# FFN of a convolution-attention block: first layer as two fp16 products of split, DMA-turned rows, with the bias in ScalarE's copy

## The reference, cut to what matters

```
t = t + attn(ln(t))                      # gives x2
h = clip-scale(ln(t) @ sign(W1 - mean).T + b1)   # 96 -> 384, five groups of the batch
h = gelu(h)
t = t + clip-scale(h @ sign(W2 - mean).T + b2)   # 384 -> 96, five groups of the batch
```

## Time and profile before

| what | value |
|---|---|
| three runs | 2713.96, 2716.24, 2720.21 us, median 2716.24 |
| profiled execution | 2713.15 us, of which the trace spans 2711.4 us |
| mean granted TensorE clock | 0.977 |
| busy, share of the span | TensorE 93%, VectorE 78%, ScalarE 72%, GpSimd 56% |
| DMA bytes | 290.84 MB, mean 107 GB/s |

### The profile page before, as it was taken

The page is one execution under the profiler, slowest core; times in us unless marked ns, Lnnn a source line. Parts: engine busy times, 40 slices in busy tenths (PEclk is TensorE's granted clock), DMA queues, the critical chain, the costliest instruction groups (busy, mean ns, idle before and its releaser), DMA issues. The chain is left out here.

```text
span 2711.4 us, 83212 instructions
## 1 busy us (share of the span) xinstructions
PE 2534.1 (93%) x29309; PEld 1505.9 (56%) x29309; DVE 2103.7 (78%) x3025; ACT 1956.5 (72%) x3751; POOL 1509.3 (56%) x2545
## 2 busy tenths in 40 slices
PE   4899999999999959999999999999999997899996
PEld 2555555555555525666666666666666654455553
DVE  3577676666767448999999999999999975779997
ACT  2687777877777627777777777777777773677775
POOL 0133342333334247888888888888888871225445
PEclk9999999999999969999999999999999998999998
DMA  1122322323222246666666666666666634334546
GB/s 37 30 88 70 95 80 73 101 70 104 70 87 87 82 116 116 120 127 127 121 128 125 123 128 123 127 125 122 127 127 119 128 71 127 97 112 135 147 135 164
DMA packets 777485, 290.84 MB, mean 107 GB/s; under 512 B 702865, under 2 KB 760498, under 8 KB 777394
## 3 DMA queue, kind: packets, MB, share of 16 engines
q1 hardware_dynamic: 776050, 288.43, 46.6%
q10 hardware_dynamic: 1344, 1.18, 0.1%
HBM read 100.77 MB, written 87.29 MB: 69 GB/s over the span
## 5 line engine op out<-in xcount | busy, mean ns | idle before, releaser
L1034 DVE TENSOR_REDUCE at_row_max<-at_ps_queries 128x1 f32<-128x1024 f32 (+7 forms) x1536 | 1067.4, 745 | 103.9 <-PE at_ps_queries L917 103.9
L990 ACT ACTIVATE at_probs<-at_ps_keys 128x512 f32<-128x512 f32 x1344 | 720.8, 596 | 236.8 <-PE at_ps_keys L932 236.5
L907 PE MATMUL at_ps_queries<-at_turned 48*128 48x512 f16 (+3 forms) x2304 | 608.7, 332 | 58.5 <-DVE at_row_max L1034 36.4
L932 PE MATMUL at_ps_keys<-at_turned 50*128 50x128 f16 (+3 forms) x3456 | 574.8, 273 | 6.2 <-ACT at_diag_probs L990 0.5
L952 PE MATMUL at_ps_values<-at_probs,at_v 128*32 128x128 f32 x10752 | 413.8, 278 | 0.5 <-DVE at_out L1026 0.4
L932 PEld LDWEIGHTS at_ps_keys<-at_turned 50*128 50x128 f16 x3456 | 230.1, 94 | 195.0 <-ACT at_probs L990 74.4
L851 POOL TENSOR_TENSOR at_recip<-at_out,at_minus_one 128x8 f32<-128x8 f32 x192 | 313.7, 1634 | 2.8 <-DVE at_out L1026 2.8
L952 PEld LDWEIGHTS at_ps_values<-at_probs,at_v 128*32 128x32 f32 x10752 | 258.7, 109 | 89.9 <-issue 73.3
L513 POOL TENSOR_TENSOR cb_o_hat<-cb_o,cb_o_scale 128x768 f32<-128x768 f32 x32 | 48.0, 1501 | 461.5 <-DVE cb_o_scale L433 461.5
L990 ACT ACTIVATE at_diag_probs<-at_ps_keys 128x512 f32<-128x512 f32 x384 | 230.8, 601 | 35.9 <-PE at_ps_keys L932 27.7
L915 PE MATMUL at_ps_queries<-mask_queries,shifted 64*128 64x256 bf16 (+1 forms) x960 | 241.9, 252 | 0.0
(11 more groups left out here) (223 smaller groups left out, 5078.1 us busy)
## 6 DMA issues: line engine op xcount, KB each, us to landing
qkv_rows<-cb_packed SPq DMA_DIRECT2D x32, 1152.0 KB, 7.6
at_stacks<-qkv_rows SPq DMA_DIRECT2D x192, 192.0 KB, 2.9
cb_x<-in_x_dram SPq DMA_DIRECT2D x32, 384.0 KB, 3.7
cb_x_again<-in_x_dram SPq DMA_DIRECT2D x32, 384.0 KB, 4.5
x_after_conv<-cb_x SPq DMA_DIRECT2D x32, 384.0 KB, 5.0
ff_att_rows<-attention_rows SPq DMA_DIRECT2D x32, 384.0 KB, 4.3
ff_x<-x_after_conv SPq DMA_DIRECT2D x128, 96.0 KB, 2.3
x_after_attention<-ff_x SPq DMA_DIRECT2D x30, 384.0 KB, 2.9
```

The source lines that it names most:

```text
L907: mm = pe.matmul(scores[:, c0:c0 + width], QT[Q_ROWS, slot, qb * P:(qb + 1) * P], KT[Q_ROWS, slot, k0 * P:k1 * P], start=(c0 == 0), stop=True,
L932: mm = pe.matmul(pk[:, bank_k, c0:c0 + n * P], KT[K_ROWS, slot, kb * P:(kb + 1) * P], QT[K_ROWS, slot, q0 * P:(q0 + n) * P], start=(c0 == ...
L990: act.activation(probs, pk[:, ring(r, u + (u > MAX_TURN)), :], ACT.Exp, scale=scale).then_inc(S["probs"], 1)
L1034: ins = dve.tensor_reduce(MX[:, (r - 3) % 2, qb:qb + 1], pq[:, (NR * (r - 1) + g) % QBUFS, b0 * P:(b0 + n) * P], AX.X, ALU.max)
```

## The change

The float32 product becomes two fp16 ones. The sign weights are stored in fp16. GpSimd scales the normalised rows by 256 more than before (`XN_UNIT`, put in through the variance), copies them to fp16, subtracts that copy from the float32 rows and stores the remainder in fp16 too. A DMA transpose on SyncE's queue turns both parts; the eight TensorE transposes and ScalarE's copy of them go. The two parts are multiplied by the same weights into the same PSUM bank. b1 leaves the product and enters ScalarE's copy as a bias, with the scale 1/256. Everything ahead of the first layer runs one turn earlier (n = r + 3, m = r + 2).

```
-    w["w1"] = sb("w1", [C + 1, HIDDEN])
+    w["w1"] = sb("w1", [C, HIDDEN], FP16)
+    w["b1"] = sb("b1", [P, CHUNKS])
...
-        XNT = sb("xn_t", [C + 1, L])
+        XP = sb("xn_parts", [P, 2, TILES, P], FP16)
+        XNT = sb("xn_t", [P, 2, 2, TILES, P], FP16)
...
+                    if 0 <= x < FULL:            # SyncE, x = r + 1, behind the x2 store
+                        sp.wait_ge(S["xn_ready"], x + 1)
+                        _above(sp.wait_ge, S["y1_psum"], 6 * (x - 1))
+                        sp.dma_start_transpose(XNT[:, x % 2, :, :, :].rearrange("p m t n -> p (m t) n"),
+                                               XP[:, :, :, :].rearrange("p m t n -> p (m t n)")
+                                               ).then_inc(xn_turned[x % 2], 16)
...
-                        pe.matmul(pf[:, a * BANK:(a + 1) * BANK], w["w1"][:, k * P:(k + 1) * P],
-                                  XNT[:, a * BANK:(a + 1) * BANK], start=True, stop=True).then_inc(S["y1_psum"], 1)
+                        for part in range(2):
+                            tokens = XNT[0:C, n % 2, part, :, :].rearrange("p (e u) n -> p u e n", e=2)
+                            mm = pe.matmul(pf[:, a * BANK:(a + 1) * BANK], w["w1"][:, k * P:(k + 1) * P],
+                                           tokens[:, 2 * a:2 * a + 2, :, :], start=(part == 0), stop=(part == 1))
+                        mm.then_inc(S["y1_psum"], 1)
...
-                    if 0 <= r < FULL:
-                        pe.wait_ge(S["xn_ready"], r + 1)
-                        pe.wait_ge(S["att_copied"], min(r + 3, BATCH))
-                        for t in range(TILES):
-                            mm = pe.transpose(pt[0:C, t * P:(t + 1) * P], XN[:, t % 2 * 4 + t // 2, :], w["ident"][:, :])
-                        mm.then_inc(S["xn_turned"], 1)
...
-                                       ACT.Copy).then_inc(S["y1_copied"], 1)
+                                       ACT.Identity, bias=w["b1"][:, k:k + 1], scale=1.0 / XN_UNIT
+                                       ).then_inc(S["y1_copied"], 1)
...
-                        act.wait_ge(S["xn_turned"], r + 1)
-                        act.activation(XNT[0:C, :], pt[0:C, :], ACT.Copy).then_inc(S["xnt_ready"], 1)
...
                         pool.tensor_tensor(XN[:, :, :], XC[:, :, :], _bcast(SCALE[:, :], 2, C), ALU.mult
+                                           ).then_inc(S["xn_made"], 1)
+                        pool.wait_ge(S["xn_made"], m + 1)
+                        _above(pool.wait_ge, xn_turned[(m - 1) % 2], 16 * ((m + 1) // 2))
+                        pool.tensor_copy(XP[:, 0, :, 0:C], XN[:, :, :]).then_inc(S["xn_high"], 1)
+                        pool.wait_ge(S["xn_high"], m + 1)
+                        pool.tensor_tensor(XP[:, 1, :, 0:C], XN[:, :, :], XP[:, 0, :, 0:C], ALU.subtract
                                            ).then_inc(S["xn_ready"], 1)
```

More of the change, by code:

```diff
@@ L137, in prepare @@
             (w2_raw[:, :], A["L1_ffn_W2"]),
-            (w["w1"][C:C + 1, :], A["L1_ffn_b1"].rearrange("(a n) -> a n", a=1)),
+            (w["b1"][:, :], A["L1_ffn_b1"].rearrange("(k p) -> p k", p=P)),
             (lng[:, :], A["L0_conv_ln_g"].rearrange("(n a) -> n a", a=1)),
@@ L1048, in project_and_ffn @@
     LIMIT = QB - QEPS
+    XN_UNIT = 256.0
     FULL = GROUPS * GB
@@ L1077, in project_and_ffn @@
         G1, G2 = sb("max1", [P, 2, GB * CHUNKS]), sb("max2", [P, 2, GB])
-        ROW = sb("row_of_ones", [1, P])
+        ROW = w["fc1"][0:1, 0:P]
         M1, M2 = sb("group_max1", [P, GROUPS, 4]), sb("group_max2", [P, GROUPS, 4])
@@ L1101, in project_and_ffn @@
         stored = [sem(f"stored{i}") for i in range(4)]
-        names = ("ones_set half_set att_turned att_copied y_done x2_ready x2_turned x2_sums centred squares var_sums scale xn_ready "
-                 "xn_turned xnt_ready y1_psum y1_copied y1_max max1 all_max1 scale1 gelu h_ready y2_psum y2_ready "
+        xn_turned = [sem(f"xn_turned{i}") for i in range(2)]
+        names = ("ones_set half_set att_turned att_copied y_done x2_ready x2_turned x2_sums centred squares var_sums scale xn_made xn_high xn_ready "
+                 "y1_psum y1_copied y1_max max1 all_max1 scale1 gelu h_ready y2_psum y2_ready "
                  "y2_max max2 all_max2 scale2 limited limited_late out_ready").split()
@@ L1124, in _ @@
                 load_x1(1)
-                for r in range(-2, FULL + OUT_LAG):
-                    n, s = r + 2, r - OUT_LAG
+                for r in range(-3, FULL + OUT_LAG):
+                    n, s, x = r + 3, r - OUT_LAG, r + 1
                     if n < BATCH:
@@ L1158, in _ @@
             def _(pe):
-                pe.wait_ge(S["ones_set"], 2)
+                pe.wait_ge(S["ones_set"], 1)
                 def hidden(n, k):
@@ L1184, in _ @@
                 turn_att(0)
-                for r in range(-2, FULL + LAG + 1):
-                    n, m, s = r + 2, r + 1, r - LAG
-                    if 0 <= r < FULL:
-                        pe.wait_ge(S["xn_ready"], r + 1)
-                        pe.wait_ge(S["att_copied"], min(r + 3, BATCH))
-                        for t in range(TILES):
-                            mm = pe.transpose(pt[0:C, t * P:(t + 1) * P], XN[:, t % 2 * 4 + t // 2, :], w["ident"][:, :])
-                        mm.then_inc(S["xn_turned"], 1)
+                for r in range(-3, FULL + LAG + 1):
+                    n, m, s = r + 3, r + 2, r - LAG
                     if 0 <= m < FULL:
@@ L1214, in _ @@
                     if 0 <= r < FULL:
-                        pe.wait_ge(S["xnt_ready"], r + 1)
+                        pe.wait_ge(xn_turned[r % 2], 16 * (r // 2 + 1))
                         hidden(r, 0)
@@ L1282, in _ @@
                         act.wait_ge(S["centred"], m + 1)
-                        act.activation(SQ[:, :, 0:C], XC[:, :, :], ACT.Square, scale=C ** -0.5).then_inc(S["squares"], 1)
+                        act.activation(SQ[:, :, 0:C], XC[:, :, :], ACT.Square, scale=C ** -0.5 / XN_UNIT).then_inc(S["squares"], 1)
                     if 0 <= r < FULL:
@@ L1306, in _ @@
                 pool.memset(MINUS_HALF[:, :], -0.5).then_inc(S["half_set"], 1)
-                pool.memset(SQ[:, :, C:C + 1], 1e-5).then_inc(S["half_set"], 1)
+                pool.memset(XP[:, :, :, C:P], 0.0)
+                pool.memset(SQ[:, :, C:C + 1], 1e-5 / XN_UNIT ** 2).then_inc(S["half_set"], 1)
                 pool.wait_ge(S["half_set"], 2)
-                for r in range(-1, FULL + OUT_LAG):
-                    m, o = r + 1, r - OUT_LAG
+                for r in range(-2, FULL + OUT_LAG):
+                    m, o = r + 2, r - OUT_LAG
                     if 0 <= o < FULL - GB and o % GB == 0:
@@ L1314, in _ @@
                         pool.wait_ge(S["var_sums"], m + 1)
-                        _above(pool.wait_ge, S["xn_ready"], m)
+                        _above(pool.wait_ge, S["xn_made"], m)
                         pool.tensor_tensor(SCALE[:, :], VS[:, :], MINUS_HALF[:, :], ALU.pow).then_inc(S["scale"], 1)
                         pool.wait_ge(S["scale"], m + 1)
-                        _above(pool.wait_ge, S["xn_turned"], m)
                         pool.tensor_tensor(XN[:, :, :], XC[:, :, :], _bcast(SCALE[:, :], 2, C), ALU.mult
+                                           ).then_inc(S["xn_made"], 1)
[4 more added lines that the diff above has]
+                        pool.tensor_tensor(XP[:, 1, :, 0:C], XN[:, :, :], XP[:, 0, :, 0:C], ALU.subtract
                                            ).then_inc(S["xn_ready"], 1)
@@ L1357, in peak1 @@
                                       apply_absolute_value=True).then_inc(S["y1_max"], 1)
-                for r in range(-2, FULL + OUT_LAG):
-                    n, m, s, o = r + 2, r + 1, r - LAG, r - OUT_LAG
+                for r in range(-3, FULL + OUT_LAG):
+                    n, m, s, o = r + 3, r + 2, r - LAG, r - OUT_LAG
                     if o >= 0 and o % GB == 0:
@@ L1371, in _ @@
                         dve.wait_ge(S["x2_sums"], m + 1)
-                        _above(dve.wait_ge, S["xn_ready"], m)
+                        _above(dve.wait_ge, S["xn_made"], m)
                         for a in range(2):
```

1 line of the change is left out of this document (removed).

## The result

| | before | after |
|---|---|---|
| median (lowest to highest) | 2715.10 us (2712.02 to 2720.21) | 2684.98 us (2679.37 to 2687.19) |
| profiled execution, span | 2713.15, 2711.4 us | 2682.86, 2681.1 us |
| mean granted TensorE clock | 0.977 | 0.967 |

The ratio is 0.9884, 95% interval 0.9861 to 0.9907. The forecast was 2677.0 us within 2657 to 2709: the range holds the result and the sign was right; the gain is 30 us where 39 were forecast.

The account below looks back on a forecast made before the run. TensorE was taken to bound the main stretch at 13.44 us a turn. Gains of 12.3, 12.8 and 18.5 less 5 us at the start make 39 us: 2674 profiled, 2677 us as median, range 2657 to 2709.

Parts of the forecast that it names:

- TensorE: Main-stretch turn: eight transposes (1.01 us) go and the first layer falls to 2.7 us, leaving 9.7 of 13.44 us.
- rival D: First layer on TensorE: an fp16 pass no faster than a float32 record, only 1.0 us a turn gained, 2699 us; chance 0.03.
- ScalarE: Each turn: bias in six copies adds 0.54 us, a copy of about 1.0 goes; loop with TensorE 11.6 to 11.7 us.
- Items 7 to 14: Seven turns with no output yet, from 13.63 to 11.8 us each: a gain of 12.8 us.
- VectorE and GpSimd: From item 14 on, VectorE bounds 15 turns: 13.63 to 12.4 us each, 0.1 of it for contention; gain 18.5 us.
- Rival A: From item 14 on, GpSimd's longer work slows VectorE fully: 13.4 us a turn, 2693 us in all; chance 0.18.
- The first stretch: Items 0 to 7: single buffer XP sets 9 us, clock adds 1.2, so 10.2 against 11.96 a turn; gain 12.3 us.
- The start: First item goes through two GpSimd operations and the DMA instead of transposes and copy: 5 us more, once.
- The transpose in the main stretch: SyncE's transposing DMA, 4.6 us to landing against 7.0 us of room in a turn: hidden, costs nothing.
- rival C: SyncE's transpose lands late behind 768 KB of loads and stores: slower, 2740 us; chance 0.07.
- Rival B: TensorE, less busy, is granted 1.2 GHz once a turn: 13.3 us a turn, 2708 us in all; chance 0.12.
- The drain: End of the kernel: the drain keeps its work, so the change costs nothing there.

Follow-up runs that it names:

- e4: The kernel after, with ScalarE's first-layer copies made without the bias (b1 left out): 2680.92 us, ratio 0.9878 to the kernel before.
- e12: The kernel after, with the transpose first in SyncE's turn and GpSimd's copy waiting for VectorE's three limits: 2661.26 us, ratio 0.9797 to the kernel before.
- e14: The kernel after, with GpSimd's copy waiting for VectorE's limits and the transpose between attention-row load and x2 wait: 2657.63 us, ratio 0.9798 to the kernel before.
- e1: The kernel after, with two buffers for the split parts and four slots instead of six for tiles read again: 2715.58 us, ratio 1.0006 to the kernel before.
- e3: The kernel after, with two buffers for the split parts and the transpose first in SyncE's turn: 2693.44 us, ratio 0.9922 to the kernel before.
- e2: The kernel after, with the transpose first in SyncE's turn, ahead of loads, x2 wait and store: 2693.24 us, ratio 0.9926 to the kernel before.
- e13: The kernel after, with only a wait added: GpSimd's copy of the high part waits for VectorE's three limits: 2674.70 us, ratio 0.9860 to the kernel before.

## Why the prediction was right, and where it was not

- **TensorE.** Right in its main term: the pitch of an fp16 product is 0.22 us, rival D's 0.45 is out. TensorE is busy 87% of 2437 to 2600 us, not near 80%: it works in groups of four products with waits between, each with the whole 0.38 us of one record in it, and the clock was 0.95. How much each of the two adds is not separated.
- **ScalarE.** Right: copies at 0.69 us, the loop at 11.62. e4 shows the price of the bias in each copy, and a shorter turn only from item 8 to 14.
- **Items 7 to 14, forecast 12.8, gained 8.4 us.** The step that failed took all seven turns as full ones. The first, in which the GELUs begin, took 88.3 - 6 x 11.61 = 18.6 us; before, the first product of item 8 came at 2362.60, 15.1 us behind item 7's. The chain of the kernel after there:

```profile
2340.78 3.24 ACT ff_hidden L1267 x3
...
2347.43 0.68 ACT ff_hidden L1260
...
2348.16 1.89 PE ff_ps_hidden L1176 x4
2350.05 5.84 PE ff_ps_out L1247 x72
...
2355.91 1.21 ACT ff_ffn L1282 x3
```

It goes once through GELUs, a limit, sums, centring, squares and a copy before item 7's last products, and the first second layer takes 5.84 us at a granted clock of 0.70, where it took 4.02 in a turn of the earlier trace rows. A shorter first layer shortens little of that. This one turn took 6.8 us more than the 11.8 put down for it; the other six took 1.1 less in all.
- **VectorE and GpSimd, forecast 18.5, gained 15.5 us.** The turn took 187.8 / 15 = 12.5 us, forecast 12.4, so the term of 0.1 us for contention was nearly right in this kernel. That is less insight than it looks: it sits between 12.0 (e12 to e14) and 13.9 (e1 to e3), by whether GpSimd's copy falls on the limits. Rival A (13.4 a turn) has the right mechanism, and without the wait for the transpose it comes about and goes past its size (13.9); in this kernel that wait kept the copy away, which the prediction did not see. So that this term came near is in good part luck. The Trainium skill ("GPSIMD Engine Reference", Key points) has VectorE and GpSimd contend over a shared interface for VectorE instructions in a two-port mode or with two SBUF inputs; the runs agree: limit (0.70 to 1.36 us) and output (0.94 to 1.78) stretch, the reductions stay at 0.94 and 1.21.
- **The first stretch, forecast 12.3, gained 14.5 us.** The size was near by luck, the reason wrong. I let the single buffer set 9 us a turn. The stretch alternates turns of 8.0 to 8.9 and 10.8 to 12.0 us, and it is SyncE's place of the transpose, behind the wait for x2, that makes the long ones: e1 took nothing away, e2 took 10 us. I had listed what the transpose delays on SyncE, and not what delays the transpose.
- **The start, forecast -5, was -7.2 us.** The same step: the parts of item 0 were ready at 2264.07, the transpose left at 2266.04. In e2 item 0's first product comes 3.6 us earlier (2267.90 against 2271.55).
- **The transpose in the main stretch.** Hidden, as forecast: all five of TensorE's waits for it (17.6 us on the row of its products) are in the first stretch; rival C is out. But it was also waited for by GpSimd (28.1 us in 13 turns), and that wait turned out to be useful: e1 and e2, without it, lost 20 us.
- **The clock.** Rival B, one fall in every turn of the main stretch, is out: 0.95 granted there as a whole. But it is there in part, where the forecast had nothing: two of the last fifteen turns at 0.77, each with 2.0 us of idle VectorE time behind it, about 4 us. The 1.2 us a turn for it in the first stretch was of the right kind: 0.78 granted, and keeping TensorE busy gave 2.5 us of the 8.4 put down for seven turns.
- **The drain, forecast 0, cost 1.0 us.** One second layer there took 5.78 us in place of 4.09, at a granted clock of 0.70, behind a wait of 2.6 us.

## What to carry to other kernels

When a change takes the bound away from one engine, the next engine's time can depend on where its instructions lie beside those of its neighbour, and not only on their count: look up which instruction each slow one overlaps, and try a wait that holds the engine with slack back until they have passed (by the ratios 6.5 us in e13, 35 in e12 against e2). And for a DMA that is put into a queue, ask first what stands ahead of it in program order, then what it holds up.

## What was not expected of the hardware

- An earlier landing made the kernel slower: 10 us gained in the first seven turns, 2.4 lost in the next seven and 19.5 in the last fifteen (e2).
- The stretching goes both ways, but not for all pairs: the cast goes from 0.82 to 1.44 us and the cap from 2.85 to 3.80 beside limits, while GpSimd's product of the rows stays at 1.47 us beside the output, which alone pays (0.94 to 1.78). Why one pair shares the cost and the other does not, no run here shows.
- The same transposing DMA of 512 KB costs SyncE 1.9 us to issue (median) and lands in 4.4 us where it goes out first in the turn (e2), 3.5 and 5.5 us behind the loads and the store (the kernel after).
